# Attention, gated scan and mixture of experts on one core: key stack by quarter, constants spread over groups, last pair sums on VectorE

## What is computed

```python
def xattn(x, k, v, w_proj, b_proj):          # 16 heads of 32
    q = x.reshape(B, T, H, d) * scale; k = k.reshape(B, S, H, d) * scale
    w = softmax(einsum('bthd,bshd->bhts', q, k))
    return einsum('bhts,bshd->bthd', w, v).reshape(B, T, W) @ w_proj.T + b_proj

def scan_layer(x, norm_w, W_in, b_in, W_x, b_x, W_dt, b_dt, W_out, b_out):
    xn = x * rsqrt(mean(x * x) + EPS) * norm_w
    u, z, g = split(xn @ W_in + b_in, 3)
    ut = tanh(u @ W_x + b_x); dt = sigmoid(z @ W_dt + b_dt)
    h = gated_scan(a=1 - dt, b=dt * ut)       # h[t] = a[t] h[t-1] + b[t]
    return x + (h * sigmoid(g)) @ W_out + b_out

def ffn(x, ...):                              # 8 experts, top 2, and two shared ones
    scores = softmax(x @ gate_w.T); idx = top_k(scores + gate_bias, 2)
    y = sum over e of gate_e * ((silu(x @ w1[e].T) * (x @ w3[e].T)) @ w2[e].T)
    return y + (silu(x @ sw1.T) * (x @ sw3.T)) @ sw2.T

x = x + xattn(layernorm(x), ctx, ctx, ...)
x = x + scan_layer(layernorm(x), ...)
return x + ffn(layernorm(x), ...)
```

## Time and profile before

| | us |
|---|---|
| median of 3 runs | 533.91 (533.06 to 534.15) |
| the profiled execution, whole | 533.72 |
| its span | 531.9 |
| TensorE busy | 469.6 (88%) |
| VectorE busy | 404.7 (76%) |
| ScalarE busy | 326.8 (61%) |
| GpSimd busy | 290.4 (55%) |

### The profile page before, as it was taken

One profiled execution on the slowest core, in us unless ns is written; L12 is line 12 of the kernel. 1 busy time (PEld: TensorE's weight loads), 2 busy tenths in 40 slices (PEclk: granted clock), 3 DMA queues, 4 the chain that ended last, 5 costly groups with the idle time before them and its releaser, 6 DMA issues.

```text
span 531.9 us, 15785 instructions
## 1 busy us (share of the span) xinstructions
PE 469.6 (88%) x6731; PEld 328.7 (62%) x6731; DVE 404.7 (76%) x598; ACT 326.8 (61%) x362; POOL 290.4 (55%) x274
## 2 busy tenths in 40 slices
PE   0468789998999999999989945999999999999994
PEld 0125556666767667767666533844878788787642
DVE  3467577877877788787762798698599999999426
ACT  3327466776676687676654473456579888888320
POOL 1047499988999999999769430482001101010032
PEclk9999899999999999999999986999999999999998
DMA  6986799998889988987991831086999999997125
GB/s 194 249 194 204 183 258 275 245 242 227 229 241 267 264 256 211 243 225 183 371 407 52 297 112 47 1 265 247 415 358 411 417 418 416 416 417 319 41 80 177
DMA packets 48253, 133.97 MB, mean 252 GB/s; under 512 B 6452, under 2 KB 31284, under 8 KB 37428
## 3 DMA queue, kind: packets, MB, share of 16 engines
q1 hardware_dynamic: 43928, 120.38, 70.7%
q0 software_dynamic: 3680, 12.06, 6.3%
q10 hardware_dynamic: 576, 0.52, 0.6%
HBM read 96.77 MB, written 11.01 MB: 203 GB/s over the span
## 4 chain that ended last, share of the span: by engine, by line
PE 49%; DVE 28%; issue 8%; DMA 8%; POOL 3%; ACT 3%; SPq 1%; DVEq 0%; ACTq 0%; POOLq 0%
PE bank L1024 10%; PE bank L1059 9%; DVE ws L805 9%; PE bank L1044 7%; DVE mx L720 7%; PE bank L1068 6%; DMA wst<-in_ffw 5%; PE bank L1184 2%; PE bank L1185 2%; PE bank L1186 2%; POOL ps L636 2%; DMA kstk<-kl 2%; DVE hf L946 1%; PE bank L1127 1%; DVE hl L951 1%
## 5 line engine op out<-in xcount | busy, mean ns | idle before, releaser
L720 DVE TENSOR_REDUCE mx<-bank 128x1 f32<-128x512 f32 x240 | 154.6, 686 | 55.0 <-PE bank L1024 52.9
L636 POOL TENSOR_TENSOR ps<-pt 128x512 f32<-128x512 f32 x128 | 159.7, 1274 | 11.4 <-ACT pt L475 6.5
L475 ACT ACTIVATE pt<-bank 128x1024 f32<-128x1024 f32 x128 | 124.1, 1023 | 60.6 <-PE bank L1044 58.8
L805 DVE SCALAR_TENSOR_TENSOR ws<-wst,ws 128x2048 f16<-128x2048 f32 x51 | 115.8, 2290 | 1.8 <-ACT ws L523 1.2
L523 ACT ACTIVATE ws<-wst 128x2048 f16<-128x2048 f32 x48 | 90.6, 1904 | 5.8 <-DMA wst<-in_ffw 5.7
L611 POOL TENSOR_TENSOR kl<-kt,kh 128x512 f16<-128x512 f32 x58 | 67.6, 1186 | 28.2 <-ACT kh L440 28.1
L1199 PE MATMUL bank<-xt,ws 128*128 128x128 f16 x480 | 81.2, 219 | 0.5 <-DVE hf L946 0.5
L1201 PE MATMUL bank<-xt,ws 128*128 128x128 f16 x480 | 81.2, 219 | 0.0
L1200 PE MATMUL bank<-xt,ws 128*128 128x128 f16 x480 | 81.2, 219 | 0.0
L1024 PE MATMUL bank<-kstk,q 96*128 96x512 f16 x176 | 69.0, 417 | 11.6 <-DMA kstk<-kl 7.1
L677 POOL DMA_DIRECT2D ys_rows<-xn x15 | 8.2, 543 | 120.9 <-ACT xn L592 120.9
(11 more groups left out here) (170 smaller groups left out, 720.0 us busy)
## 6 DMA issues: line engine op xcount, KB each, us to landing
wst<-in_ffw SPq DMA_DIRECT2D x51, 1024.0 KB, 10.6
kt<-in_keysT SPq DMA_DIRECT2D x16, 1024.0 KB, 6.0
v<-in_vals SPq DMA_DIRECT2D x16, 1024.0 KB, 9.4
kstk<-kh SPq DMA_DIRECT2D x84, 128.0 KB, 4.8
kstk<-kl SPq DMA_DIRECT2D x44, 128.0 KB, 3.3
wst<-kh SPq DMA_DIRECT2D x40, 128.0 KB, 3.6
xs_rows<-biases SPq DMA_DIRECT2D x15, 256.0 KB, 3.0
x_tok<-xs_rows POOLq DMA_DIRECT2D x15, 256.0 KB, 8.6
```

The costliest lines, as they stand in the source:

```text
L475: act.activation(pt[:, n % 4, :, :, :].rearrange("p j a t -> p (j a t)"), bank[:, 2 * (n % 2):2 * (n % 2) + 2, :].rearrange("p j n -> p (j ...
L636: pool.tensor_tensor(ps2[:, n % 4, :, :], pt[:, n % 4, 0, :, :], pt[:, n % 4, 1, :, :], ALU.add)\
L720: dve.tensor_reduce(mx[:, a, q:q + 1], bank[:, 4 + k % 2, :], AX.X, ALU.max).then_inc(m_taken, 1)
L805: dve.scalar_tensor_tensor(ws[:, home_of(q), 1, m, :, :].rearrange("p c n -> p (c n)"), wst[:, q % 2, m, :, :].rearrange("p c n -> p (c n) ...
```

## The change

It does the following.

- **Key stack.** Each stack is kept by quarter, then head, then key: `[KM, q, a, 512]`. A copy writes one run of 2048 halves (4 KB) per partition where it wrote four of 1 KB. What is copied, how often and from which partitions to which stays, and TensorE reads the same 128 or 512 columns, at other addresses. The rows of ones are filled in flattened form.
- **Constants.** Three of the 12 constants are issued in each of the turns 4 to 7 instead of all in turn 13, and one of the first three weights in each of the turns 8, 9 and 10 instead of all in turn 14.
- **`b_proj`** is added by GpSimd in the groups 13 and 14 (two batches in each, after the third and the sixth pair sum), and `zero` is cleared right after.
- **Last group.** VectorE makes the 8 pair sums of group 15. There it also scales `win` (after the division of group 14) and makes the constants and the router split (after the second two pair sums), and it takes `split_low(0, 0)` right after the last division. `split_low(0, 1)` stays behind the four batches.
- **Residual.** VectorE makes `x1 + xn` itself as `x1 * (1 + r) - mean * r`, with two small instructions for the factors, and GpSimd only adds `b_out` to it.
- **ScalarE** rounds the first expert weight in group 14, the second and `wout` right after its last exponential, and asks for the sigmoid table before it waits for `uz`.

The diff:

```diff
@@ -142,5 +142,6 @@
     kl = temp("kl", [P, 2, HG, S // 4], F16)
-    kstk = temp("kstk", [KM, 2, HG, S], F16)
+    kstk = temp("kstk", [KM, 2, HG, HG, S // 4], F16)
     third = wst[0:KM, 1, :, :, :].rearrange("p m c n -> p (m c n)").bitcast(F16)[:, 0:HG * S]
-    stacks = [kstk[:, 0, :, :], kstk[:, 1, :, :], third.rearrange("p (a s) -> p a s", a=HG)]
+    stacks = [kstk[:, 0, :, :, :], kstk[:, 1, :, :, :],
+              third.rearrange("p (q a s) -> p q a s", q=HG, a=HG)]
     v = temp("v", [P, 2, J, P], F32)
@@ -238,4 +239,4 @@
     hn_done = sem("hn_done")
-    h_done = sem("h_done")
-    x1b_done = sem("x1_plus_b_out")
+    x1h_done = sem("x1_plus_normed")
+    rows_made = sem("row_factors_made")
     x2p_done = sem("x2_residual")
@@ -326,3 +327,3 @@
             for q in (2 * h, 2 * h + 1):
-                eng.dma_start(stacks[j % 3][row:row + HD, :, q * S // 4:(q + 1) * S // 4],
+                eng.dma_start(stacks[j % 3][row:row + HD, q, :, :],
                               src[q * HD:(q + 1) * HD, j % 2, :, :]).then_inc(k_rep[j % 3][h], 16)
@@ -358,4 +359,5 @@
         sp.dma_start(idh[:, :], t["idh"]).then_inc(id_in, 16)
-        sp.dma_start(kstk[KS:KM, :, :, :], t["ones"]).then_inc(ones_in, 16)
-        sp.dma_start(stacks[2][KS:KM, :, :], t["ones"][:, 0, :, :]).then_inc(ones_in, 16)
+        sp.dma_start(kstk[KS:KM, :, :, :, :].rearrange("k b q a s -> k (b q a s)"),
+                     t["ones"].rearrange("k b a s -> k (b a s)")).then_inc(ones_in, 16)
+        sp.dma_start(third[KS:KM, :], t["ones"][:, 0, :, :].rearrange("k a s -> k (a s)")).then_inc(ones_in, 16)
         sp.wait_ge(kt_in[0], 16)
@@ -385,8 +387,6 @@
                 stack(i + 3, 1)
-            if i == G - 3:
-                for dst, name in CONSTS:
-                    sp.dma_start(dst, t[name]).then_inc(consts, 16)
-            if i == G - 2:
-                for m in range(3):
-                    sp.dma_start(wst[:, 0, m, :, :], t["ffw"][0, m]).then_inc(w_in[0][m], 16)
+            for dst, name in CONSTS[3 * i - 12:3 * i - 9] if 4 <= i < 8 else []:
+                sp.dma_start(dst, t[name]).then_inc(consts, 16)
+            if 8 <= i < 11:
+                sp.dma_start(wst[:, 0, i - 8, :, :], t["ffw"][0, i - 8]).then_inc(w_in[0][i - 8], 16)
         sp.wait_ge(st_done, HS * (G - 1))
@@ -497,2 +497,12 @@
         queries_high(2)
+        def split_first(m):
+            act.wait_ge(w_in[0][m], 16)
+            if m == 0:
+                act.wait_ge(split_lo, G - 1)
+                for j in (G - 2, G - 1):
+                    for half in range(2):
+                        act.wait_ge(k_rep[j % 3][half], 16 * 6 * (j // 3 + 1))
+            act.activation(ws[:, 0, 0, m, :, :].rearrange("p c n -> p (c n)"),
+                           wst[:, 0, m, :, :].rearrange("p c n -> p (c n)"), ACT.Copy, scale=WS).then_inc(w_hi[m], 1)
+
         for i in range(G):
@@ -501,2 +511,4 @@
                     exponent(n)
+                if i == G - 2 and p == 1:
+                    split_first(0)
                 if p == 1 and i + 2 < G:
@@ -512,7 +524,2 @@
-        def split_first(m):
-            act.wait_ge(w_in[0][m], 16)
-            act.activation(ws[:, 0, 0, m, :, :].rearrange("p c n -> p (c n)"),
-                           wst[:, 0, m, :, :].rearrange("p c n -> p (c n)"), ACT.Copy, scale=WS).then_inc(w_hi[m], 1)
-
         def split_high(q, m):
@@ -536,2 +543,5 @@
+        split_first(1)
+        act.wait_ge(consts, NC)
+        act.activation(wo[:, 0, :], wout[:, :], ACT.Copy, scale=WS).then_inc(wo_hi, 1)
         for b in range(B):
@@ -542,11 +552,6 @@
                            scale=1.0 + 1e-8).then_inc(roots, 1)
-            if b == 0:
-                act.wait_ge(x1_done, 1)
-                split_first(0)
-            else:
+            if b > 0:
                 copy_normed(b - 1)
-        act.wait_ge(consts, NC)
-        act.activation(wo[:, 0, :], wout[:, :], ACT.Copy, scale=WS).then_inc(wo_hi, 1)
         copy_normed(B - 1)
-        split_first(1)
+        act.activation(r1[:, 0, 0:2], eps[:, :], ACT.Sigmoid)
         act.wait_ge(uz_ready, 2)
@@ -638,9 +643,8 @@
-        def add_bias():
+        def add_bias(b):
             pool.wait_ge(xn_done, B)
             pool.wait_ge(consts, NC)
-            for b in range(B):
-                pool.tensor_tensor(x[:, b, :], x[:, b, :], bproj[:, :], ALU.add).then_inc(xb_done, 1)
+            pool.tensor_tensor(x[:, b, :], x[:, b, :], bproj[:, :], ALU.add).then_inc(xb_done, 1)
-        for i in range(G):
+        for i in range(G - 1):
             for hs in range(HS):
@@ -654,3 +658,4 @@
                     queries_low(i + 3)
-        add_bias()
+                if i in (G - 3, G - 2) and hs in (2, 5):
+                    add_bias(2 * (i - G + 3) + hs // 3)
         pool.wait_ge(xb_done, B)
@@ -658,8 +663,4 @@
         for b in range(B):
-            pool.wait_ge(x1_done, b + 1)
-            pool.tensor_tensor(x2[:, b, :], x1[:, b, :], bout[:, :], ALU.add).then_inc(x1b_done, 1)
-        for b in range(B):
-            pool.wait_ge(h_done, b + 1)
-            pool.wait_ge(x1b_done, b + 1)
-            pool.tensor_tensor(x2[:, b, :], x2[:, b, :], xn[:, b, :], ALU.add).then_inc(x2p_done, 1)
+            pool.wait_ge(x1h_done, b + 1)
+            pool.tensor_tensor(x2[:, b, :], x2[:, b, :], bout[:, :], ALU.add).then_inc(x2p_done, 1)
@@ -784,5 +785,25 @@
+        def split_low(q, m):
+            dve.wait_ge(w_hi[m], q + 1)
+            dve.scalar_tensor_tensor(ws[:, home_of(q), 1, m, :, :].rearrange("p c n -> p (c n)"),
+                                     wst[:, q % 2, m, :, :].rearrange("p c n -> p (c n)"), WS,
+                                     ws[:, home_of(q), 0, m, :, :].rearrange("p c n -> p (c n)"),
+                                     ALU.mult, ALU.subtract).then_inc(w_lo[m], 1)
+
+        def make_constants():
+            dve.wait_ge(one_set, 2)
+            dve.tensor_scalar(starts[:, :], iota[:, :], float(P), None, ALU.mult)
+            link(dve.tensor_tensor_scan(upper[:, :], one[:, :], idf[:, :], 0.0, ALU.mult, ALU.add))
+            dve.tensor_tensor(trih[:, 0, :], upper[:, :], idf[:, :], ALU.subtract).then_inc(tri_done, 1)
+            link(dve.tensor_copy(gwh[:, :, 0:E], gwt[:, :, :]))
+            dve.tensor_tensor(gwh[:, :, E:2 * E], gwt[:, :, :], gwh[:, :, 0:E], ALU.subtract).then_inc(gw_split, 1)
+
+        def pair_sum(n):
+            dve.wait_ge(add_done, n)
+            dve.wait_ge(exp_done, n + 1)
+            dve.wait_ge(den_done, n - 3)
+            dve.tensor_tensor(ps2[:, n % 4, :, :], pt[:, n % 4, 0, :, :], pt[:, n % 4, 1, :, :], ALU.add)\
+                .then_inc(add_done, 1)
+
         for i in range(G):
-            if i == G - 1:
-                scale_win()
             for p in range(HS // 2):
@@ -790,2 +811,5 @@
                     take_max(j, k)
+                if i == G - 1:
+                    for n in (HS * i + 2 * p, HS * i + 2 * p + 1):
+                        pair_sum(n)
                 if p == 0 and i > 0:
@@ -797,2 +821,6 @@
                     shift(i + 1)
+                if i == G - 1 and p == 0:
+                    scale_win()
+                if i == G - 1 and p == 1:
+                    make_constants()
                 if p in (1, 2) and i == 0:
@@ -801,9 +829,3 @@
         divide(G - 1)
-
-        def split_low(q, m):
-            dve.wait_ge(w_hi[m], q + 1)
-            dve.scalar_tensor_tensor(ws[:, home_of(q), 1, m, :, :].rearrange("p c n -> p (c n)"),
-                                     wst[:, q % 2, m, :, :].rearrange("p c n -> p (c n)"), WS,
-                                     ws[:, home_of(q), 0, m, :, :].rearrange("p c n -> p (c n)"),
-                                     ALU.mult, ALU.subtract).then_inc(w_lo[m], 1)
+        split_low(0, 0)
@@ -819,13 +841,9 @@
                 .then_inc(hn_done, 1)
-            dve.tensor_scalar(xn[:, b, :], x1[:, b, :], mv[:, b, 0:1], lnv[:, 2, b:b + 1], ALU.subtract, ALU.mult)\
-                .then_inc(h_done, 1)
-        dve.wait_ge(one_set, 2)
-        dve.tensor_scalar(starts[:, :], iota[:, :], float(P), None, ALU.mult)
-        link(dve.tensor_tensor_scan(upper[:, :], one[:, :], idf[:, :], 0.0, ALU.mult, ALU.add))
-        dve.tensor_tensor(trih[:, 0, :], upper[:, :], idf[:, :], ALU.subtract).then_inc(tri_done, 1)
+            link(dve.scalar_tensor_tensor(r1[:, 1, b:b + 1], mv[:, b, 0:1], -1.0, lnv[:, 2, b:b + 1], ALU.mult, ALU.mult))
+            dve.tensor_scalar(r1[:, 2, b:b + 1], lnv[:, 2, b:b + 1], 1.0, None, ALU.add).then_inc(rows_made, 1)
+            dve.wait_ge(rows_made, b + 1)
+            dve.tensor_scalar(x2[:, b, :], x1[:, b, :], r1[:, 2, b:b + 1], r1[:, 1, b:b + 1], ALU.mult, ALU.add)\
+                .then_inc(x1h_done, 1)
         dve.wait_ge(wo_hi, 1)
         dve.scalar_tensor_tensor(wo[:, 1, :], wout[:, :], WS, wo[:, 0, :], ALU.mult, ALU.subtract).then_inc(wo_lo, 1)
-        link(dve.tensor_copy(gwh[:, :, 0:E], gwt[:, :, :]))
```

(6 more changed lines are left out.)

## The result

The changed kernel took **539.79 us** in the median of six runs (535.01 to 544.46), the kernel before 533.57 beside it. The longest of the six is a slow run, which the ratio leaves out. The ratio is 1.011, with an interval from 1.0066 to 1.0153. Twelve more runs later, beside other kernels, gave 535.68 and a ratio of 1.0035 (0.9998 to 1.0071). The forecast was 528.0, so it was wrong by 8 to 12 us and in its sign. The profiled execution took 535.01, its span is 533.1.

A forecast was written before the change was run, and what follows sets the result against it. Steady attention (TensorE, GpSimd) and experts (TensorE, VectorE, DMA) were taken as full, so only three joints could pay: 533.7 - 1.0 (start) - 4.9 (to the scan) + 0.2 (constants) = 528.0 us; range 522.8 to 531.0.

The forecast's parts named there:

- Constants: Loads moved into turns 4 to 10 of attention: taken as 0, up to 0.6 us kept as a cost.
- 4.6 us of slack: Attention, values of group 6: landing at 140.0, needed at 144.59; loads of 2.6 us in turns 5 to 10 fit within.
- a wait for `v` in group 6: Sign of a wrong forecast: TensorE waiting in group 6 of attention for values; no size given.
- a steady group that isn't 15.0 us: Sign in attention: steady groups were to keep 15.0 us; any other length would upset the whole sum.
- slow copies: Rival, key stack copies get slower: at 140 GB/s a group takes 16.4 us, the kernel 546; chance 0.06.
- Key stack: Copies at the start: rate nearly kept, 210 to at best some 220 GB/s; 1.0 us off.
- fast copies: Rival, long runs make the key stack copies fast: 4.2 us off the start instead of 1.0, 524.4; chance 0.27.
- Last group: End of attention: VectorE's sums end at 286.2, denominators about 287.1, so the projection begins 0.4 us earlier.
- the third rival: VectorE late in the last group: sums end at 291.8, `x1` 3.3 us later than forecast, 531.3; chance 0.11.
- First batch: After the projection: `x1` starts at 290.7, 1.3 us earlier, of which 0.8 is kept.
- way to the scan: Up to the scan: `dt`, not VectorE, is late next; `scan_a` at 310.75, gated output at 314.9, 4.9 us earlier.
- The rest: From the scan to the end: chain to the experts unchanged, full stretch moves as a whole, nothing given back.

The follow-up runs named there:

- late loads: Changed kernel with first weight and constants in turn 13 behind the values, two weights in turn 14, `b_proj` adds behind the last pair sum: 529.74 us, ratio 0.9921.
- late weights: Changed kernel with only the three weights moved, to turns 13 and 14, constants staying in turns 4 to 7: 533.29 us, ratio 0.9973.

## Why the prediction was wrong

*Constants: the step that failed.* It took 0 for the loads, kept up to 0.6 as a cost, and put 0.2 into the sum. They cost 6 to 10 us in timed runs (535.7 or 539.8 against 529.7 with late loads) and 6.0 to 8.2 in the profiles (excess 6.8 to 9.0 against 0.8). The step had the numbers in hand: it compared 2.6 us of load with "4.6 us of slack" of the values. But that slack is a latency of one transfer, and it is used up once, while the load of each turn takes room out of the same 15 us. By the prediction's own rates a turn with a weight asks for 7.5 us of copies and 7.8 for 3.15 MB, 15.3 of 15.0. That the engines would be full could be read there; that full engines move only some 270 to 300 GB/s of the mixture, so that a turn takes 16.7 to 17.6 us, could not.

*Its signs.* The prediction named "a wait for `v` in group 6" and "a steady group that isn't 15.0 us" as what would upset it. Both came, and the larger ones stood in groups 10 and 11, at which it had not looked. No rival had this mechanism; the one on the other side, slow copies, was the wrong way to the same full queue.

*Key stack: no rival came true, but the size is not shown.* The first maximum matmul came at 19.1 to 22.9, median 20.5, in fifteen profiles with the new layout and at 20.3 to 22.2, median 21.5, in five with the old one. The medians differ by 1.0 us, as taken, but the ranges overlap for the most part, and the kernel with nothing but the new layout had it at 22.33; so that the number agrees may be luck. The copies' stretch 16:19 moved 239 GB/s instead of 212, with runs four times as long:

```profile
16.00:19.00 3.00, 0.00 (x0) 0.00 (x0) 1.39 (x4) 1.49 (x2) 0.00 (x0) 1.00 1.12 239
```

So fast copies fall (their sign was a first matmul before 18.5), and slow copies too. The Trainium skill (SBUF — State Buffer, "Door 1: The DMA port swizzle") gives about 218 GB/s for transfers over 32 such partitions; 239 is a little over it, but this stretch holds parts of the values' load too, issued at 15.8, so the row does not refute the rule. What the last steps expected, that a gain at the start goes through whole, is not shown: in timed runs the layout alone gave 0.0 us (0.9973 to 1.0037).

*Last group: mis-sized.* Forecast 0.4 shorter, measured 0.5 longer (15.0 against 14.5), with 14.8 to 15.1 in all kernels with this edit. A sum took 0.69 us as forecast, the scaling 1.1 to 1.5 for 1.0, the constants about 1.1 for 1.3. In the changed kernel the last sum ends at 290.75, 13.85 after the last shift, where the forecast has 13.3 (286.2 - 272.93) and GpSimd had needed 14.1. The sum of the step left out that VectorE stands idle between the first sums, for an exponential and for denominators. No denominator waits for a sum there. TensorE's longest stop there is again one at an instruction without a semaphore; that it makes the group longer is read from the trace and not tested:

```profile
287.89 0.62 PE L1077 MATMUL bank<-pt,v 128*32 128x128 f32 x16
289.61 0.64 PE L1077 MATMUL bank<-pt,v 128*32 128x128 f32 x16 [1.10 <-issue]
```

All nine profiles with the adds of `b_proj` in groups 13 and 14 have it, at the same place and with 0.8 to 1.2 us. In the six that have the adds later it is not there, but GpSimd then adds beside VectorE's first two sums: in the kernel with late loads they take 0.98 and 1.66 us, the last sum ends at 284.96, 14.7 after the shift, and the denominators wait for it:

```profile
282.09 2.87 DVE L808 TENSOR_TENSOR ps<-pt 128x512 f32<-128x512 f32 x4
```

```profile
282.84 0.43 PE L1089 MATMUL bank<-ps,ones 128*32 128x128 f32 x8 [0.36 <-DVE ps L808]
283.56 0.42 PE L1089 MATMUL bank<-ps,ones 128*32 128x128 f32 x8 [0.30 <-DVE ps L808]
```

So the third rival came true in the kernel with late loads, at a fraction of its price of 3.3, and not in the changed one.

*First batch and way to the scan: right.* From the projection to the product with `scan_wo` it took 28.1 us in every kernel with the edit, 32.4 without; forecast 27.9. Its parts stand in the rows above: `x1` behind TensorE, 0.55 for each `hn`, VectorE ready before `dt`. `split_low` took 3.36 us, 1.1 over its price, in the slack that the step had found for it.

*The rest: nearly.* Behind the product the times agree within 0.3 us up to the first `hf` but for the clock (below); from there to the end they are 187.6 to 190.1 in the twenty profiles without order; the runs don't show why.

With the loads late the whole comes near the forecast, 4.2 us off by the ratio against 5.9, but in part by luck. Piece by piece, its profile is 1.1 shorter than the one before up to the first maximum matmul, 1.6 in groups 5 to 14 (the kernel before had lost that much in group 5, where its own stop stands) and 4.3 in the front; it is 0.6 longer in the last group and 2.2 behind the product. The forecast had neither the 1.6 nor the 2.2.

## What to carry to other kernels

Before a transfer is moved beside others, add up the bytes of the whole period and divide by what the engines make of that mixture when full; a latency that looks like slack pays for one transfer, and a queue remembers. A load belongs behind what is needed next, and if it can't stand there, the urgent transfer goes ahead: a swap of two issues gave back 4 to 8 us here by the medians. When a load is moved, look at each instruction that waits for it, and at what stands behind that instruction.

## What the runs showed of the chip

A short wait of TensorE costs more than itself once the granted clock falls. Waits for `v` of 1.11 and 1.54 us made their groups 1.2 and 1.8 us longer, and one of 1.69 made its group 1.7 longer; behind these the 32 products took 1.1 to 1.2 us. Waits of 1.70 and 1.71 made 3.3 and 3.4, and 2.17 to 2.56 made 3.7 to 4.2; behind these the 32 products took 1.8 to 1.9 us. In the kernel with late weights the granted clock behind such a wait is 0.50 of full, the lower of the levels of 1.2 and 2.4 GHz. The first row, with 0.56, is a mean that takes in the last of the time at full clock:

```profile
160.00:162.00 2.00, 1.84 (x32) 1.50 (x32) 0.00 (x0) 0.00 (x0) 2.00 (x3) 0.56 0.90 200
160.30:163.60 3.30, 3.30 (x42) 2.52 (x38) 0.69 (x1) 0.09 (x1) 3.30 (x4) 0.50 1.02 218
```

The clock's return differs between executions of one kernel. After the waits of the scan TensorE works at 0.50; in the first profile of the changed kernel it is back at full about 15 us behind the product with `scan_wo`, in the second nearly 20, with the same work. In three of twenty profiles it is back after 19.7 or 19.8 us, and they take 26.0 to 26.1 us to the first `hf`; in the others, back after 13.2 to 15.8, it is 23.9 to 24.2. So the late return goes with all of the 1.9 us. The stretch from 14 to 16 us behind the product in the first profile, in which the clock comes back, and that from 16 to 18 in the second, in which it has not:

```profile
334.04:336.04 2.00, 2.00 (x54) 1.79 (x52) 0.00 (x0) 1.01 (x2) 2.00 (x3) 0.71 0.00 0
```

```profile
337.95:339.95 2.00, 2.00 (x15) 1.44 (x13) 1.45 (x5) 1.38 (x2) 2.00 (x2) 0.50 0.03 8
```

A sum takes longer beside another engine's: VectorE's pair sum takes 0.69 us alone and 1.66 us beside GpSimd's adds, which then take 1.7 us instead of 1.27.

How much the same kernel moves between two sets of runs was larger than I had taken it to be: 539.8 in six runs and 535.7 in twelve, with waits for `v` in all four profiles.
